# A graph attention layer on one core: float32 scores on two 64-row tiles in place of a high/low split

## The reference

```python
h = jnp.maximum(_layernorm(x, axis=-1), 0.0)
adj = jnp.maximum(adjacency_matrix, eye)
q = jnp.einsum('nd,hdk->hnk', node_matrix, Wqs)
k = jnp.einsum('nd,hdk->hnk', node_matrix, Wks)
v = jnp.einsum('nd,hdk->hnk', node_matrix, Wvs)
scores = jnp.einsum('hqk,hmk->hqm', q, k) * kd ** (-0.5)
scores = scores + IDENTITY_BIAS * eye - MASK_VAL * (1.0 - adj)
att = jax.nn.softmax(scores, axis=-1)
return jnp.einsum('hqm,hmk,hko->qo', att, v, Wo)
```

## Time and profile before

| | |
|---|---|
| median of 3 runs | 3127.39 us (3122.81 to 3129.61) |
| profiled execution, span | 3131.2 us |
| TensorE busy | 3056.8 us (98%) |
| VectorE busy | 2444.3 us (78%) |
| ScalarE busy | 2171.6 us (69%) |
| GpSimd busy | 492.8 us (16%) |
| granted clock of TensorE | nine tenths or more in all 40 slices |

### The profile page before, as it was taken

How to read it: one execution, slowest core, us unless ns; L and a number is a source line. 1 busy time by engine, 2 the same in 40 slices (tenths; PEclk the granted TensorE clock), 3 DMA queues, 4 the chain that set the end, 5 groups by cost and what they waited for, 6 DMA issues and landing times.

```text
span 3131.2 us, 58791 instructions
## 1 busy us (share of the span) xinstructions
PE 3056.8 (98%) x18368; PEld 1892.8 (60%) x18368; DVE 2444.3 (78%) x4345; ACT 2171.6 (69%) x3297; POOL 492.8 (16%) x658
## 2 busy tenths in 40 slices
PE   7999999999999999999989999999999999999998
PEld 5566666666666666666556655666665666565664
DVE  6778788887878887887557877878877778777775
ACT  3677777777777777777547767767777667677675
POOL 3011111101111110111001111111111111111110
PEclk9999999999999999999999999999999999999999
DMA  5234444433444443344424433444433444433442
GB/s 154 53 85 88 95 79 98 84 81 78 91 91 84 94 85 85 73 95 87 94 74 80 88 84 73 87 93 81 93 79 72 86 94 81 93 79 72 89 93 52
DMA packets 217847, 267.82 MB, mean 86 GB/s; under 512 B 57472, under 2 KB 176768, under 8 KB 217728
## 3 DMA queue, kind: packets, MB, share of 16 engines
q1 hardware_dynamic: 173568, 178.51, 24.6%
q0 software_dynamic: 41984, 83.91, 16.1%
q10 hardware_dynamic: 2176, 4.19, 0.4%
HBM read 169.87 MB, written 12.71 MB: 58 GB/s over the span
## 4 chain that ended last, share of the span: by engine, by line
PE 92%; DVE 3%; issue 3%; DMA 1%; SPq 1%; DVEq 0%; ACT 0%; POOL 0%; POOLq 0%
PE psS L383 31%; PE psO L406 23%; PE psT L396 21%; PE psO L417 10%; PE psP L368 2%; PE psS L341 2%; DVE S L631 1%; PE psP L426 1%; PE psO L356 1%; PE psP L356 1%; DVE PT L645 1%; DMA S<-in_x 1%; SPq L239 0%; DMA S<-hT_scratch 0%; PE psT L327 0%
## 5 line engine op out<-in xcount | busy, mean ns | idle before, releaser
L631 DVE CUSTOM_DVE_ANT_0 S<-psS,B 128x1024 f32<-128x1024 f32 x1024 | 1239.6, 1211 | 169.0 <-PE psS L383 151.5
L517 ACT ACTIVATE S<-S,negm 128x1536 f32<-128x1536 f32 (+1 forms) x768 | 1094.8, 1427 | 62.9 <-DVE negm L638 59.7
L524 ACT ACTIVATE PT<-psT 128x512 f32<-128x512 f32 x768 | 457.0, 595 | 656.0 <-PE psT L396 654.3
L406 PE MATMUL psO<-PT,V 128*64 128x256 f32 x5120 | 836.0, 405 | 0.0
L396 PE MATMUL psT<-ident,S 128*128 128x128 f32 x5120 | 797.6, 283 | 31.4 <-DVE PT L645 24.3
L396 PEld LDWEIGHTS psT<-ident,S 128*128 128x128 f32 x5120 | 566.2, 141 | 398.2 <-issue 293.6
L383 PE MATMUL psS<-K,QH 128*128 128x512 f32 x2048 | 738.3, 442 | 8.4 <-DVE mx L631 5.9
L383 PE MATMUL psS<-K,QL 128*128 128x512 f32 x2048 | 643.8, 395 | 0.0
L645 DVE COPY PT<-psT 128x512 f32<-128x512 f32 x512 | 352.7, 689 | 332.4 <-PE psT L396 292.1
L658 DVE STREAM_TRANSPOSE S<-S 128x1536 f32<-128x1536 f32 x256 | 454.0, 1773 | 38.0 <-PE psO L417 37.9
L406 PEld LDWEIGHTS psO<-PT,V 128*64 128x64 f32 x5120 | 254.1, 135 | 362.4 <-issue 248.6
(11 more groups left out here) (52 smaller groups left out, 1056.1 us busy)
## 6 DMA issues: line engine op xcount, KB each, us to landing
S<-S SPq DMA_DIRECT2D x1536, 96.0 KB, 2.2
B<-in_adj POOLq DMA_DIRECT2D x256, 256.0 KB, 5.4
hq<-hT_scratch SPq DMA_DIRECT2D x32, 256.0 KB, 3.2
RB<-rden_scratch SPq DMA_DIRECT2D x128, 64.0 KB, 3.2
S<-in_x SPq DMA_DIRECT2D x8, 512.0 KB, 3.6
hT_scratch<-S ACTq DMA_DIRECT2D x8, 512.0 KB, 4.1
acc<-in_x POOLq DMA_DIRECT2D x16, 256.0 KB, 4.5
partial_scratch<-res POOLq DMA_DIRECT2D x16, 256.0 KB, 3.2
```

The source lines that it names most:

```text
L406: last = nc.tensor.matmul(psO[a * KD:(a + 1) * KD, 0:QW], V[:, 2 * s + a, h * KD:(h + 1) * KD], PT[:, s % RING, a * QW:(a + 1) * QW], star ...
L517: nc.scalar.activation(part, part, ACT.Exp, bias=negm[:, h % 2, q:q + 1], accum_out=sums[:, h % 2, q, e:e + 1]).then_inc(probs_ready, 1)
L524: nc.scalar.activation(PT[:, s % RING, :], psT[s % 2][:, :], ACT.Copy).then_inc(pt_act, 1)
L631: nc.vector.tensor_tensor_reduce(out=part, in0=psS[j % 2][:, :], in1=B[:, q, k * SLOT:(k + 1) * SLOT], scale=SCALE, scalar=LOWEST, op0=ALU ...
```

## The change

Scores become plain float32. K has no low part: a head's keys of the even chunks lie in rows 0 to 63 and those of the odd chunks in rows 64 to 127, Q is held in both halves, and a slot is two float32 matmuls with 64 rows, 128 columns of weights and 512 moving columns, one in each half of the array and each into its own bank. `query` makes both halves of Q at once, with 4 matmuls where there were 2, and one copy takes them. B is float32, and GpSimd adds the 0.01 on the diagonal to it once for each block (L637 goes). The halves of psO are no longer summed: one multiplication takes all 128 rows, and `project` has Wo in both halves and runs 4 matmuls where there were 2, each adding over both. V(0) waits for that multiplication. All 16 late moves go by DMA. ScalarE takes slots 0, 1, 2, 4, 5, 6, 8, 9, VectorE slots 3 and 7. The order of TensorE's step is T(2c) T(2c+1) S(c+2) V(2c-2) V(2c-1).

```diff
-ACT_SLOTS = [0, 2, 4, 6, 8, 9]
-DVE_SLOTS = [1, 3, 5, 7]
+ACT_SLOTS = [0, 1, 2, 4, 5, 6, 8, 9]
+DVE_SLOTS = [3, 7]
...
-                    if qi != qj:
-                        src, dst = late_blocks(h, qi, qj)
-                        sp.dma_start(dst, src).then_inc(late_moved, 16)
+                    src, dst = late_blocks(h, qi, qj)
+                    sp.dma_start(dst, src).then_inc(late_moved, 16)
...
-            nc.gpsimd.tensor_tensor(own, own, notI[:, :], ALU.mult).then_inc(bias_ready, 1)
+            nc.gpsimd.tensor_tensor(own, own, notI[:, :], ALU.mult).then_inc(bias_conv, 1)
+            wait_apart(pool, bias_conv, i * (2 * QT) + 2 * q + 2, pool_passed)
+            nc.gpsimd.tensor_tensor(own, own, diag[:, :], ALU.add).then_inc(bias_ready, 1)
...
-            for c in range(DC):
-                last = nc.tensor.matmul(query_psum(first)[:, 0:QW], wq[:, c, h * KD:(h + 2) * KD], hq[:, c, :],
-                                        start=(c == 0), stop=(c == DC - 1))
+            for e in range(2):
+                for c in range(DC):
+                    last = nc.tensor.matmul(query_psum(first)[:, e * QW:(e + 1) * QW],
+                                            wq[:, c, h + e, :, :].rearrange("p e k -> p (e k)"), hq[:, c, :],
+                                            start=(c == 0), stop=(c == DC - 1))
...
-            for part, hi in ((QH, True), (QL, False)):
-                for b in range(SLOT // BANK):
-                    col = k * SLOT + b * BANK
-                    last = nc.tensor.matmul(psS[j % 2][:, b * BANK:(b + 1) * BANK], part[:, h, q * P:(q + 1) * P],
-                                            K2[:, h, col:col + BANK], start=hi, stop=not hi)
+            for r in range(2):
+                rows = slice(r * KD, (r + 1) * KD)
+                last = nc.tensor.matmul(psS[j % 2][:, r * BANK:(r + 1) * BANK], Q[rows, h, q * P:(q + 1) * P],
+                                        K[rows, h, k * BANK:(k + 1) * BANK], start=True, stop=True)
...
             for q in range(QT):
-                last = nc.tensor.matmul(psP[:, q * D:(q + 1) * D], O[:, q * P:(q + 1) * P], wo[:, h // 2, :], start=True, stop=True)
+                for e in range(2):
+                    last = nc.tensor.matmul(psP[:, q * D:(q + 1) * D], O[:, e, q * P:(q + 1) * P], wo[:, h - 1 + e, :],
+                                            start=(e == 0), stop=(e == 1))
...
                 transposes(i, h, 2 * c)
+                transposes(i, h, 2 * c + 1)
                 if nxt:
                     scores(i1, h1, c + 2)
...
                 if c:
                     values(i, h, 2 * c - 2)
-                transposes(i, h, 2 * c + 1)
-                if c:
                     values(i, h, 2 * c - 1)
...
-                own = S[:, h % 2, q, bass.ds(i * QW + q * P, P)]
-                nc.vector.tensor_tensor(own, own, diag[:, :], ALU.add)
...
-            nc.vector.tensor_tensor(Oodd[:, :], psO[0:KD, 0:QW], Oodd[:, :], ALU.add).then_inc(o_summed, 1)
+            dve.wait_ge(late_used, count(i, h, 1, 1))
             dve.wait_ge(rden_in, count(i, h, 16, 16))
             dve.wait_ge(projected, count(i, h, 1, START - h % 2))
-            nc.vector.tensor_tensor(O[half_ * KD:(half_ + 1) * KD, :].rearrange("k (q p) -> k q p", q=QT),
-                                    Oodd[:, :].rearrange("k (q p) -> k q p", q=QT),
+            nc.vector.tensor_tensor(O[:, h % 2, :].rearrange("k (q p) -> k q p", q=QT),
+                                    psO[:, 0:QW].rearrange("k (q p) -> k q p", q=QT),
                                     RB[:, :].rearrange("k (p q) -> k q p", q=QT), ALU.mult).then_inc(o_ready, 1)
```

More of the change, by code:

```diff
@@ L50 @@
 QUAD = P // 32
-MOVES = QUAD * (QUAD - 1)
+MOVES = QUAD * QUAD
 RING = 4
@@ L291, in constants @@
             pool.wait_ge(ones_set, 3)
-            for m, fill in ((ident, 1.0), (notI, 0.0), (diag, IDENTITY_BIAS)):
+            for m, fill in ((ident, 1.0), (notI, 0.0), (diag, IDENTITY_BIAS / SCALE)):
                 nc.gpsimd.affine_select(out=m[:, :], in_=m[:, :], compare_op=ALU.not_equal, fill=fill, base=0,
@@ L490, in keys_values @@
         def keys_values(i, b, nxt, nxt2):
-            for h in range(GROUP):
-                act.wait_ge(k_proj, i * GROUP + (b * (GROUP // 2) + h // 2 + 1))
-                rows = slice(h % 2 * KD, (h % 2 + 1) * KD)
-                nc.scalar.activation(K2[0:KD, h, bass.ds((i * 2 + b) * CH, CH)], psK[h // 2][b][rows, :], ACT.Copy).then_inc(k_hi, 1)
+            act.wait_ge(k_proj, i * GROUP + (b * (GROUP // 2) + 1))
+            for h in range(2):
+                last = nc.scalar.activation(K[b * KD:(b + 1) * KD, h, bass.ds(i * CH, CH)], psK[0][b][h * KD:(h + 1) * KD, :],
+                                            ACT.Copy)
+            last.then_inc(k_act, 2)
             if norm and nxt:
@@ L501, in keys_values, with take_query @@
                                  ACT.Copy).then_inc(v_act, 1)
[L503 removed]
+        def take_query(i, h, first=False):
             act.wait_ge(q_proj, count(i, h, 1, 2))
[L506 to L510 removed]
+            nc.scalar.activation(Q[:, h:h + 2, :], query_psum(first)[:, :].rearrange("p (e n) -> p e n", e=2),
+                                 ACT.Copy).then_inc(q_ready, 2)
         def exps(i, h, q, e):
@@ L596, in keys_values @@
                 normalise(*after(i, b))
-            for h in range(GROUP):
-                if h == 2 and norm and nxt2:
-                    statistics(i + 1, b)
-                dve.wait_ge(k_hi, i * (2 * GROUP) + (b * GROUP + h + 1))
-                rows = slice(h % 2 * KD, (h % 2 + 1) * KD)
-                cols = bass.ds((i * 2 + b) * CH, CH)
-                nc.vector.tensor_tensor(K2[KD:2 * KD, h, cols], psK[h // 2][b][rows, :], K2.bitcast(F32)[0:KD, h, cols],
-                                        ALU.subtract).then_inc(k_lo, 1)
-            if not nxt:
-                for e in range(2):
-                    query_lo(0, 0, e, True)
+            if norm and nxt2:
+                statistics(i + 1, b)
+            dve.wait_ge(k_proj, i * GROUP + (b * (GROUP // 2) + 2))
+            for h in range(2, GROUP):
+                last = nc.vector.tensor_copy(K[b * KD:(b + 1) * KD, h, bass.ds(i * CH, CH)],
+                                             psK[1][b][(h - 2) * KD:(h - 1) * KD, :])
+            last.then_inc(k_dve, 2)
             dve.wait_ge(v_proj, i * 4 + (2 * b + 2 + START))
@@ L610, in keys_values @@
                                   psV[1][:, :].rearrange("p (a n) -> p a n", a=2)).then_inc(v_dve, 1)
-        def query_lo(i, h, e, first=False):
-            dve.wait_ge(q_hi, count(i, h, 1, 2))
-            for half_ in range(2):
-                rows = slice(half_ * KD, (half_ + 1) * KD)
-                last = nc.vector.tensor_tensor(QL[rows, h + e, :], query_psum(first)[e * KD:(e + 1) * KD, 0:QW],
-                                               QH.bitcast(F32)[rows, h + e, :], ALU.subtract)
-            last.then_inc(q_lo, 1)
         def mask(i, h, j, first=False):
```

106 lines of the change are left out of this document (39 added, 67 removed).

## The result

The changed kernel takes 3305.45 us (median of 4 runs, 3303.48 to 3308.01), against 3128.19 us before, measured beside it. The ratio is 1.0568, with a 95% interval of 1.0553 to 1.0583: slower by 177 us. I had forecast 3278 us, slower by 151, with a range of 3140 to 3375.

What follows compares the result with a forecast made beforehand. TensorE's program and the waits put into it were taken as the bound. From a 3131.2 us span: +180 for steps, -24 for block turns, -5 for starts, 3282; less 3.8 for the median, 3278 us, range 3140 to 3375.

Steps and rivals of the forecast that it cites:

- What bounds the kernel: Whole kernel: TensorE, busy 3056.8 of 3131.2 us, bounds it; work leaving ScalarE and VectorE is worth nothing.
- The price of a block, and a border as a term of its own: TensorE's steps: pure block times plus 0.15 to 0.20 us at each change between matmul shapes.
- Side by side: Scores slots: two row halves of the array overlap, 0.86 us pure and 1.06 with border, not 1.72 pure.
- The wait at T(3): Every step: T(3) waits 0.9 us for ScalarE's copy of slot 1, bounds 0.6 and 1.2.
- SP's queue. ... Nothing: Late moves by DMA: sixteen take 10.2 us for twelve's 7.66; no cost unless the last takes over 3 us to land.
- Nothing in the sum: GpSimd's bias preparation: 4.2 us of room covers the diagonal and loads up to 3 us longer; otherwise up to 60 us.
- The turn of the block: Block turns of group 1: TensorE's 24.3 us of waits for VectorE's copies become hidden, -24 us, bounds -24 and 0.
- The clock: TensorE's clock stays at 2.4 GHz, granted nine tenths or more in every slice; waits up to 1.9 us lowered none.
- Starts: Starts: first query by one copy for 8 pieces, fewer for keys, more TensorE matmuls; -5 us, bounds -15 and +3.
- Profile against median: Whole kernel: the median lies 3.8 us below the profiled span, so a span of 3282 us gives 3278.

Runs made afterwards that it cites:

- e3: The changed kernel with both float32 matmuls of a scores slot reading rows 0 to 63, in one half of the array; 4056.59 us in one run.
- e1: The changed kernel with ScalarE copying slot 1 ahead of its exponential of 1536 columns, not behind it; 3227.85 us, ratio 1.0297.
- e2: The changed kernel with slot 1 copied by VectorE again, TensorE's order kept; 3279.28 us, ratio 1.0476.
- e4: The changed kernel with TensorE's order of before, T(2c) S(c+2) V(2c-2) T(2c+1) V(2c-1); 3340.53 us, ratio 1.0669.
- e11: The changed kernel with nothing but the bias in bfloat16 again; 3285.02 us, ratio 1.0503.
- e9: The kernel before with the changed kernel's order of TensorE and nothing else; 3181.5 us, ratio 1.0178.
- e8: The kernel before with the changed kernel's TensorE order and division of slots, and ScalarE's slot 1 ahead of the exponential; 2965.13 us, ratio 0.9486.
- e10: e8 with the change's float32 scores on two 64-row tiles, no high and low parts; 3047.64 us, ratio 0.975.
- e6: e1 with the four moves that stay on their partitions done by ScalarE again, 12 by DMA; 3157.76 us, ratio 1.0099.
- e5: e1 with the bias in bfloat16 again, 256 KB for a load instead of 512; 3172.68 us, ratio 1.0151.

## Why the prediction was right, and where it was off

- **What bounds the kernel.** TensorE's program and the waits put into it: right. 368 and 447 us of work taken off the two other engines moved nothing.
- **The price of a block, and a border as a term of its own.** Right. All blocks came out within 0.01 us, among them three that no row of before showed: scores on 64 rows, and transposes and `project` behind them. The steps came out 0.06 us longer each than worked out: +183 for +180.
- **Side by side.** The choice of 0.86 over 1.72 from the column halves was the step with most at stake, and right: the changed kernel has 1.06, e3 1.91, with the borders.
- **The wait at T(3).** Right in place and size: 0.9 forecast, 0.94 by e1. The cause was named in part: I laid it to slot 1's move to ScalarE, but on VectorE 0.50 us of it stay (e2), and with the old order of TensorE it goes but for 2.1 us in 4 places (e4). The list of waits has only 92 us of the 120, since it counts TensorE's idle time and not that the four transposes behind the stop take 0.66 us where 0.44 stands without one.
- **"SP's queue. ... Nothing", and "Nothing in the sum" for GpSimd.** This is the step that failed. I had named both: the last move issued at 11 us, and that over 3 us to land would make S(7) wait; and bias loads up to 3 us longer. I had looked at each against its own reader and not at one against the other. The loads share the DMA engines with the moves in the step of head 2, the moves land late, and mask 5 and S(7) wait for them. It cost 20 us (e11, and +21 in the account above).
- **The turn of the block.** -24 forecast, -36 measured with the small ones, and the reason that I gave for it isn't what happened: VectorE's delay is not hidden in the changed kernel, it isn't there. That the 24 us went all the same was luck. Of the other 12, some 7 are what the lower clock cost behind five of the waits, which I had priced by the list of waits alone. e9 shows what the delay costs where nothing covers it.
- **The clock.** The sign that I gave, nine tenths or more in every slice, holds, and e9's page shows it too; but the sentence that waits up to 1.9 us had not lowered a slice hid five falls to 1.2 GHz in the kernel before.
- **Starts.** -5 forecast, +2 measured with the ends of the groups. What the lighter copies gained I have not separated from TensorE's added matmuls.
- **Profile against median.** I took 3.8 us off the span, as before stood to its median. The changed kernel's median lies 4.5 us over its span: 8 us of the miss.

Steps +3, moves +21, turns -12, starts +7, and these 8 make 27, the whole of the miss. Without the 12 of the turns it would have been 39.

The parts of the change can also be laid one on the other; this sum is partly measured and partly argued. It starts from e8, which has none but the order and the slots. 2965 us; the float32 scores +83 (e10, measured), 3048; the doubled query and `project`, 0.86 us in 62 and 1.06 us in 64 steps, +121 by their blocks, 3169 (worked out, not run), between e6's 3158 and e5's 3173, which have all this and either the moves or the bias of before; both together 3228 (e1, measured); ScalarE's order, +77, 3305. What made up for part of it is the order of TensorE, 1.2 us a step, which all of these have.

## What to carry to other kernels

Price a block on TensorE by its pure passes plus the border to its neighbour, both from the chain in order of time: a change that halves the passes of one block can lose it all at its borders, and a reordering that removes borders can be worth more than a cheaper matmul. When blocks are moved together, ask for each what it waits for and when that engine can have it ready: here the order alone made the kernel 54 us slower; with two copies given to the engine that has room, the first of them ahead of its long exponential, it made it 160 us faster. Where two DMA streams grow in the same stretch, check their sum against the reader with the least room; a wait that seems hidden may be hidden only by another wait. Price a wait of TensorE not by the list of waits alone: look at the granted clock of the stretch behind it, which a page of 40 slices averages away.

## What the runs showed of the hardware

- Two float32 matmuls of 64 rows each, one in each row half of the array, cost 0.86 us for 2 x 512 columns; in the same half 1.71. Two row halves give the same overlap as the column halves of the V blocks, also with the full 128 columns of weights.
- Going between transposes and 64-row float32 matmuls costs 0.15 to 0.20 us, though both use all 128 columns (1.02 for eight transposes behind them, 0.87 behind float32r scores of 128 rows). The Trainium skill says in "TensorEngine Tiling (Array Packing)", Tiling Modes, that a change of mode drains the engine. The trace agrees in that such a change costs time for rows as for columns.
- The granted clock fell to 1.2 GHz for a few microseconds behind single waits of TensorE: behind 1.74 to 1.87 us in the kernel before (5 of 13 long turns, 1.4 us each), 1.8 to 2.6 in e1 (9 steps, 14 us), 3.9 to 4.3 in e9 (all 13 turns, 24 us). Waits of the same length also passed without a fall (1.46 to 1.87 us before, up to 2.4 in the changed kernel). On the pages of these kernels all 40 slices show nine tenths or more.
- VectorE stood 2.6 to 3.1 us, with nothing that its next copy needed missing, at 13 block turns of group 1 in the kernel before and in e9, and at none of group 0.
- Late moves of 96 KB landed in 2.2 us by the median and in 9.3 us at most with bias loads of 512 KB in the same step; the most was 6.0 us with loads of 256 KB.
